# Query squares with their bias columns in two loads, and ctx of pair 1 loaded ahead of transposed ctx of pair 2

## The reference

```python
# x (8, 64, 256), ctx (8, 1601, 256)
q, k, v = ln(x) @ Wq + bq, ctx @ Wk + bk, ctx @ Wv + bv
x = x + softmax(q @ k.T / 16) @ v @ Wo + bo
Q, K, V = ln(x) @ Wq2.T + bq2, ln(x) @ Wk2.T + bk2, ln(x) @ Wv2.T + bv2
x = x + softmax(causal(Q @ K.T / 16)) @ V
h = ln(x)                                   # 512 tokens in all
raw = h @ centroids.T                       # 8 scores a token
top = the 2 experts with the largest sigmoid(raw + routing_bias)
w = softmax(sigmoid(raw)[top])
out = x + h + shared(h) + sum(w_e * expert_e(h) for e in top)
```

## Time and profile before

| | us |
|---|---|
| median of 3 runs | 250.69 |
| lowest and highest run | 250.62, 250.86 |
| span of the profiled execution | 249.0 |
| PE busy in it | 242.5 |
| DVE, ACT, POOL busy | 154.1, 138.0, 53.0 |

### The profile page before, as it was taken

The page is one execution under the profiler, slowest core; times in us unless marked ns, Lnnn a source line. Parts: engine busy times, 40 slices in busy tenths (PEclk is TensorE's granted clock), DMA queues, the critical chain, the costliest instruction groups (busy, mean ns, idle before and its releaser), DMA issues.

```text
span 249.0 us, 5101 instructions
## 1 busy us (share of the span) xinstructions
PE 242.5 (97%) x1892; PEld 209.2 (84%) x1892; DVE 154.1 (62%) x369; ACT 138.0 (55%) x274; POOL 53.0 (21%) x82
## 2 busy tenths in 40 slices
PE   8999999989999999999998999999999999999994
PEld 8757366456367599999998999999999999999994
DVE  1752363534645887789759247766676776667683
ACT  3435132052152788796776266666666666666641
POOL 3400000000100210320676002112222222136700
PEclk9999999999999999999999999999999999999999
DMA  7999999999999999940127558999998999920232
GB/s 250 417 437 416 420 396 417 398 408 420 375 388 374 320 346 437 428 184 0 68 85 240 227 195 278 357 365 352 375 371 341 371 357 348 361 90 21 53 139 84
DMA packets 14014, 74.12 MB, mean 298 GB/s; under 512 B 1540, under 2 KB 8588, under 8 KB 9644
## 3 DMA queue, kind: packets, MB, share of 16 engines
q1 hardware_dynamic: 12700, 70.59, 74.6%
q0 software_dynamic: 1008, 2.76, 3.0%
q10 hardware_dynamic: 288, 0.52, 0.6%
HBM read 67.56 MB, written 6.32 MB: 297 GB/s over the span
## 4 chain that ended last, share of the span: by engine, by line
PE 81%; DMA 12%; DVE 3%; ACT 1%; issue 1%; SPq 0%; POOL 0%; DVEq 0%; ACTq 0%
PE psum L519 68%; DMA ctx<-ctx_dram 12%; PE psum L779 7%; DVE dlo L1362 2%; PE psum L797 1%; PE psum L617 1%; PE psum L543 1%; PE psum L840 1%; PE psum L708 1%; PE psum L550 0%; ACT dhi L1006 0%; PE psum L666 0%; DVE hlo L1247 0%; SPq L341 0%; PE psum L699 0%
## 5 line engine op out<-in xcount | busy, mean ns | idle before, releaser
L519 PE MATMUL psum<-xrowT,ring 128*128 128x128 f32 x480 | 58.3, 275 | 0.0
L519 PEld LDWEIGHTS psum<-xrowT,ring 128*128 128x128 f32 x480 | 56.2, 192 | 0.0
L1362 DVE TENSOR_TENSOR dlo<-ring,dhi 128x1024 fp32r<-128x1024 f32 x30 | 38.3, 1280 | 3.8 <-ACT dhi L1006 3.8
L1381 DVE TENSOR_TENSOR slot_hlo<-slot_h,slot_hhi 128x512 fp32r<-128x512 f32 x30 | 20.8, 692 | 29.9 <-ACT slot_hhi L1034 29.9
L1032 ACT ACTIVATE slot_h<-psum 128x512 f32<-128x512 f32 x30 | 17.9, 598 | 35.1 <-PE psum L519 35.1
L519 PE MATMUL psum<-dhi,slot_hhi 128*128 128x256 f32 x120 | 36.3, 302 | 0.1
L519 PE MATMUL psum<-dhi,slot_hlo 128*128 128x256 f32 x120 | 33.8, 282 | 0.0
L519 PE MATMUL psum<-dlo,slot_hhi 128*128 128x256 f32 x120 | 33.8, 282 | 0.0
L511 POOL DMA_INDIRECT results_dram<-y_rows,result_row x13 | 17.1, 1319 | 70.5 <-DMA results_dram<-y_rows,result_row 54.0
L1006 ACT ACTIVATE dhi<-ring 128x1024 fp32r<-128x1024 f32 x30 | 31.1, 1042 | 0.0
L519 PE MATMUL psum<-xh,parted 128*128 128x256 f32 x128 | 26.9, 288 | 0.0
(11 more groups left out here) (204 smaller groups left out, 394.0 us busy)
## 6 DMA issues: line engine op xcount, KB each, us to landing
ring<-experts_dram SPq DMA_DIRECT2D x15, 2048.0 KB, 8.0
ctx<-ctx_dram SPq DMA_DIRECT2D x4, 3072.0 KB, 28.3
ctxT_start<-ctxT_start_dram SPq DMA_DIRECT2D x4, 2048.0 KB, 20.1
ctxT_rest<-ctxT_rest_dram SPq DMA_DIRECT2D x4, 1154.0 KB, 22.4
raw<-experts_dram SPq DMA_DIRECT2D x2, 2048.0 KB, 15.9
slot_x_dram<-empty_row SPq DMA_DIRECT2D x1, 1935.0 KB, 16.3
xrow<-slot_x_dram SPq DMA_DIRECT2D x15, 129.0 KB, 7.3
squares<-squares_dram SPq DMA_DIRECT2D x1, 1285.0 KB, 14.1
```

The lines of the kernel that those rows point to most:

```text
L519: return pe.matmul(out, lhsT, rhs, start=first, stop=last)
L1362: dve.tensor_tensor(dlo[b % 2][:, steps, :], ring[b][:, steps, C * P:STEP_W], dhi[b % 2][:, steps, :].bitcast(F32), ALU.subtract).then_inc ...
L1381: dve.tensor_tensor(slot_hlo[:, half, :], slot_h[:, half, :], slot_hhi[:, half, :].bitcast(F32), ALU.subtract).then_inc(slot_hlo_ready, 1)
```

## The change

Three things are done.

1. The 13 bias and centroid columns and the two query squares become one array (`queries_dram`) and one tile (`query_start`, 1054 columns), laid out as the columns, then half k = 0 of both squares, then half k = 1. Two loads fill it: the first brings the columns and half 0 (540 columns, 270 KB), the second half 1 (514 columns, 257 KB). The load of `cols` alone, in runs of 13 values, is gone. Each half has its own semaphore, and the fold waits for half k before it multiplies half k. ACT's `spread` waits for the first.
2. SP issues both loads of `ctx` of pair 1 right after `rows`, without a wait, and `ctxT` of pairs 2 and 3 after it. Before, it was `ctxT` 2, `ctx` 1, `ctxT` 3.
3. Two tiles (`prob`, `qT`) change place in memory, and the other five squares get a tile of their own.

```diff
-        cols = sb("cols", [P, C, NCOLS])
+        query_start = sb("query_start", [P, C * NCOLS + C * 2 * (D + 1)])
+        cols = query_start[:, 0:C * NCOLS].rearrange("p (c n) -> p c n", c=C)
+        query_squares = query_start[:, C * NCOLS:].rearrange("p (k s d) -> p s k d", k=C, s=2)
...
+        def square(n, k, start, stop):
+
+            return query_squares[:, n, k, start:stop] if n < 2 else squares[:, n - 2, k, start:stop]
+
...
-            sp.dma_start(squares[:, 0:2], squares_d[:, 0:2]).then_inc(query_squares_in, 16)
-            sp.dma_start(cols[:, :, :], cols_d.rearrange("(c p) n -> p c n", p=P)).then_inc(cols_in, 16)
+            begun = C * NCOLS + 2 * (D + 1)
+            sp.dma_start(query_start[:, 0:begun], queries_d[:, 0:begun]).then_inc(query_squares_in[0], 16)
+            sp.dma_start(query_start[:, begun:], queries_d[:, begun:]).then_inc(query_squares_in[1], 16)
...
             load_ctxT(0)
-            sp.dma_start(squares[:, 2:7], squares_d[:, 2:7]).then_inc(squares_in, 16)
+            sp.dma_start(squares[:, :, :, :], squares_d).then_inc(squares_in, 16)
             load_ctxT(1)
             load_ctx(0)
             sp.dma_start(rows[:, :], rows_d.partition_broadcast(P)).then_inc(rows_in, 16)
-            for t in range(1, T - 1):
-                load_ctxT(t + 1)
-                load_ctx(t)
-            load_ctx(T - 1)
+            load_ctx(1)
+            load_ctxT(2)
+            load_ctxT(3)
+            load_ctx(2)
+            load_ctx(3)
...
-            pe.wait_ge(query_squares_in, 16)
             for k in range(C):
+                pe.wait_ge(query_squares_in[k], 16)
                 for m in range(C):
-                    ins = pe.matmul(bank(0, m * D, D), squares[:, XWQT, k, m * P:(m + 1) * P], squares[:, XWKT, k, 0:D],
+                    ins = pe.matmul(bank(0, m * D, D), square(XWQT, k, m * P, (m + 1) * P), square(XWKT, k, 0, D),
                                     start=k == 0 and m == 0, stop=k == C - 1, skip_group_check=True)
...
-            pe.wait_ge(cols_in, 16)
...
-            act.wait_ge(cols_in, 16)
+            act.wait_ge(query_squares_in[0], 16)
```

More of the change, by code:

```diff
@@ L104, in plan, with build @@
     return order
-def build(nc, x_d, ctx_d, ctx_rest_d, ctxT_start_d, ctxT_rest_d, squares_d, cols_d, rows_d, experts_d, out_d, slot_x_d, results_d):
+def build(nc, x_d, ctx_d, ctx_rest_d, ctxT_start_d, ctxT_rest_d, queries_d, squares_d, rows_d, experts_d, out_d, slot_x_d, results_d):
     with ExitStack() as whole:
@@ L190, in build @@
                            sb(f"ctxT{i}_rest", [P, 2, C, KV - 2 * BANK], F32, phase1))
-            squares = sb("squares", [P, 7, C, D + 1], F32, phase1)
+            prob = sb("prob", [P, KV], F32, phase1)
+            qT = sb("qT", [P, C, N], F32, phase1)
+            squares = sb("squares", [P, 5, C, D + 1], F32, phase1)
             aq = sb("aq", [P, C, D], F32, phase1)
@@ L198, in build @@
             product = sb("product", [P, D], F32, phase1)
-            qT = sb("qT", [P, C, N], F32, phase1)
-            prob = sb("prob", [P, KV], F32, phase1)
             probT = sb("probT", [P, KT, P], F32, phase1)
@@ L260, in build @@
         LATE_BANKS = (PO, 3, CHAIN, PT + 1)
-        x_start_in, x_rest_in, squares_in, cols_in, rows_in = (
-            sem("x_start_in"), sem("x_rest_in"), sem("squares_in"), sem("cols_in"), sem("rows_in"))
-        query_squares_in = sem("query_squares_in")
+        x_start_in, x_rest_in, squares_in, rows_in = (
+            sem("x_start_in"), sem("x_rest_in"), sem("squares_in"), sem("rows_in"))
+        query_squares_in = [sem("query_start_in"), sem("query_rest_in")]
         aq_hi, aq_lo, x1_hi, x1_lo = sem("aq_hi"), sem("aq_lo"), sem("x1_hi"), sem("x1_lo")
@@ L524, in fold_vec @@
                     for k in range(C):
-                        ins = mm(bank(b, at + m, 1), squares[:, left, k, m * P:(m + 1) * P],
+                        ins = mm(bank(b, at + m, 1), square(left, k, m * P, (m + 1) * P),
                                  cols[:, k, col:col + 1], k == 0, k == C - 1)
@@ L531, in fold_row @@
                 for k in range(C):
-                    ins = mm(bank(b, 0, D + 1), bcast[:, spread, k, :], squares[:, right, k, :], k == 0, k == C - 1)
+                    ins = mm(bank(b, 0, D + 1), bcast[:, spread, k, :], square(right, k, 0, D + 1), k == 0, k == C - 1)
                 return ins
@@ L690, in chain_v @@
                 for c in range(C):
-                    ins = mm(bank(V_BANKS[t], 0, D), xn2T[:, c, :], squares[:, AWVT, c, 0:D], c == 0, c == C - 1)
+                    ins = mm(bank(V_BANKS[t], 0, D), xn2T[:, c, :], square(AWVT, c, 0, D), c == 0, c == C - 1)
                 ins.then_inc(v_ps, 1)
@@ L720, in _ @@
                 for k in range(C):
-                    ins = mm(bank(PT, m * D, D), squares[:, XWVT, k, m * P:(m + 1) * P],
-                             squares[:, XWO, k, 0:D], k == 0, k == C - 1)
+                    ins = mm(bank(PT, m * D, D), square(XWVT, k, m * P, (m + 1) * P),
+                             square(XWO, k, 0, D), k == 0, k == C - 1)
             ins.then_inc(fold_ps, 1)
@@ L725, in _ @@
                 for k in range(C):
-                    ins = mm(bank(PT + 1, m * D, D), squares[:, AWQ, k, m * P:(m + 1) * P],
-                             squares[:, AWK, k, 0:D], k == 0, k == C - 1)
+                    ins = mm(bank(PT + 1, m * D, D), square(AWQ, k, m * P, (m + 1) * P),
+                             square(AWK, k, 0, D), k == 0, k == C - 1)
             ins.then_inc(fold_ps, 1)
@@ L730, in _ @@
             for k in range(C):
-                ins = mm(bank(PO, 0, D), bcast[:, 1, k, :], squares[:, XWO, k, 0:D], k == 0, k == C - 1)
+                ins = mm(bank(PO, 0, D), bcast[:, 1, k, :], square(XWO, k, 0, D), k == 0, k == C - 1)
             ins.then_inc(fold_ps, 1)
@@ L1457 @@
                        a["L0_attn_bq"], a["L0_attn_bk"], a["L0_attn_bv"]])
-    squares = np.concatenate([squares, beside[:, :, None]], axis=2)
+    squares = np.concatenate([squares, beside[:, :, None]], axis=2).reshape(7, C, P, D + 1)
+    cols = np.concatenate([np.stack([a["L0_xattn_bq"], a["L0_xattn_bk"], a["L0_xattn_bv"],
+                                     a["L0_attn_bq"], a["L0_attn_bk"]]), a["L0_ffn_centroids"]]).T
     ctx = a["ctx_1024"].reshape(T, 2, KV, D)
@@ L1467 @@
         "ctxT_rest_dram": ctxT[..., 2 * BANK:],
-        "squares_dram": squares.reshape(7, C, P, D + 1).transpose(2, 0, 1, 3),
-        "cols_dram": np.concatenate([np.stack([a["L0_xattn_bq"], a["L0_xattn_bk"], a["L0_xattn_bv"],
-                                               a["L0_attn_bq"], a["L0_attn_bk"]]),
-                                     a["L0_ffn_centroids"]]).T,
+        "queries_dram": np.concatenate([cols.reshape(C, P, NCOLS).transpose(1, 0, 2).reshape(P, -1),
+                                        squares[0:2].transpose(2, 1, 0, 3).reshape(P, -1)], axis=1),
+        "squares_dram": squares[2:].transpose(2, 0, 1, 3),
         "rows_dram": np.concatenate([a["L0_xattn_bo"], a["L0_attn_bv"], a["L0_ffn_routing_bias"]]),
```

## The result

| | before | changed |
|---|---|---|
| median, us (6 runs each, same chips) | 251.05 | 257.57 |
| lowest to highest | 250.62 to 251.65 | 257.07 to 258.90 |
| ratio, 95% interval | | 1.0277 (1.0257 to 1.0297) |
| span of the profiled execution, us | 249.0 | 255.6 |
| PE busy in it, us | 242.5 | 243.7 |

The account below looks back on a forecast made before the run. PE was taken as the bound, busy 242.5 of 249.0 us. Span 249.0 + 4.3 (5.0 - 0.7) + 1.6 = 254.9, with 1.7 around it 256.6 us; range 254.0 to 258.0.

Parts of the forecast that it names:

- The place in the queue: Loads of pairs 1 and 2: they land in order of issue, each after the bytes ahead, at 411 GB/s.
- The two ways to work out the landing: ctxT_start of pair 2: 48.2 from the end of the queue, 47.8 by bytes; 48.0 taken.
- less 0.4 for the shorter start: ctxT_start of pair 2: lands at 47.6 instead of 48.0 because the columns' small runs are dropped; bounds 0 and 0.6.
- The stall: Ahead of the scores of pair 2: PE has nothing to do for 5.0 us, from 4.6 to 5.6.
- The clock: Scores of pair 2 and what follows: PE's clock falls in the wait, +1.6 us, middle of 1.0 and 2.2.
- the first rival: Scores of pair 2: PE waits but its clock does not fall; 250.7 + 4.3 = 255.0 us; chance 0.24.
- The wait that goes: Weighted sum of pair 1: its ctx load has already landed, so 0.7 us of waiting is saved.
- the queue does not run dry: Issue of ctx of pair 3: some 5 us later, still before ctx of pair 2 lands at 66.97; landing stays 75.7.
- The start: Columns with query squares in two loads: the earlier first half is hidden by PE's warm-up, 0 gained.
- PE's first 11 us are as before: Start of the kernel: a sign that the changed profile shows PE unchanged there.
- cover of 0.7 us for the second half: Fold at the start: second half of the squares lands at 5.6, needed near 6.3.
- The sign on PEld: Behind the wait at the scores of pair 2: loads of 128 columns take 0.2 us, not 0.1, for a while.

Follow-up runs that it names:

- swap alone: The kernel before with only the order of loads changed, ctx of pair 1 ahead of ctxT of pair 2, and the old start; 257.89 us, ratio 1.026.
- half the bytes: The changed kernel with ctx of pair 1 in two loads of 6 chunks, one on each side of ctxT of pair 2; 251.04 us, ratio 1.0005.
- ctx between the two loads: The changed kernel with ctx of pair 1 issued between ctxT_start and ctxT_rest of pair 2; 256.61 us, ratio 1.0228.
- the busy PE: The changed kernel with 20 multiplications of the identity on PE ahead of the scores of pair 2; 255.83 us, ratio 1.0176.
- start only: The changed kernel with the old order of loads, leaving the two-part start and the tiles that changed place; 251.16 us, ratio 1.001.
- the kernel that removed that one too: The changed kernel with old load order, ctx of pair 1 split 3 chunks first, 7 warm-up multiplications, DVE's first split behind the norms; 249.86 us, ratio 0.9955.

## Why the prediction was right and where it was wrong

*The place in the queue: right; the landing 0.4 too early.* It said that the load that PE needs first lands after the bytes put ahead of it. The swap alone, half the bytes, and ctx between the two loads each moved the wait as the bytes say. The two ways to work out the landing gave 48.2 and 47.8, and their middle, 48.0, is what came: 47.97 in the changed kernel, 47.94 in the swap alone. The step that failed is "less 0.4 for the shorter start". ctxT_start of pair 0 did land 0.3 earlier (10.65 and not 10.98), but ctxT_start of pair 2 landed no earlier with the new start than with the old one. One execution of each kernel was profiled, and with the busy PE the same order of loads landed at 48.45, so a saving of 0.3 could hide in such differences; no run shows it. The scores began at 48.09 and not 47.7: that term of the sum was mis-sized by 0.4.

*The stall: too short, by 0.75.* It was put at 5.0 from PE's time at the scores before, 42.73; it was 5.75, because in this execution PE was there at 42.34. That part costs nothing, since the landing sets the end; in the sum against the earlier trace rows it cancels.

*The clock: right that it falls, the term mis-sized by 0.5.* Predicted 1.6, the middle of 1.0 and 2.2, measured 2.1. No run shows the term, or the 1.0 and 2.2 that it lies between: they are the author's estimate, made before any run had work behind a fall. In its place the runs showed a clock of 0.50 that ran on with PE at work and cost half of that work's time. In the changed kernel this was 48.09 to 52.32, 4.23 us, and the scores took 5.73 and not 3.65. In the swap alone it was 48.07 to 52.67, 4.60 us, and the same scores took 5.91, a cost of 2.3 and so over the 2.2. With ctx between the two loads it was 50.87 to 53.77, 2.90 us, and the cost was 1.4. The busy kernel, with the clock at 1.00, took 255.83 and so 0.8 more than the 255.0 of the first rival: 0.4 lies in the median of the kernel before, the rest fits a landing that came later than the 47.6 of the sum.

*The wait that goes: right.* 0.7 predicted, 0.85 between starts, of which the bracket before showed 0.67. Nothing was earned back behind, as predicted: PE's waits from 76 us on are the same one as in the earlier trace rows. But one reason given for it failed. It said that the queue does not run dry before ctx of pair 3 is issued. That issue came at 64.85, 6.6 us later than before, when little was left to move: a DMA share of 0.19 at 50 GB/s.

```profile
64.00:66.00 2.00, 1.84 (x16) 1.17 (x13) 0.48 (x1) 0.57 (x2) 0.00 (x0) 1.00 0.19 50
```

ctx of pair 3 landed at 64.85 + 11.3 = 76.15, 0.5 later than before. It cost nothing only because its user, at 86.59, stood 10 us behind.

*The start: worth nothing, as said, though it changed more than said.* The x tile came 1.0 us earlier (DVE's first statistics at 4.24 and not 5.24), which the prediction did not see; no effect on the time followed (start only: 251.16 against 251.05). SP's first load, issued at 0.77, is about half as large now, 270 KB and not 514; whether that is the reason, no run tested. And "PE's first 11 us are as before" was wrong in the profiled execution:

```profile
1.09 3.94 PEld L527 LDWEIGHTS psum<-sm 128*128 128x128 f32 x20 [1.09 <-DVE sm L1100]
...
4.24 0.43 DVE L1084 BATCH_NORM_STATS2 stats<-xs 128x6 f32<-128x256 f32 x1 [3.21 <-DMA xs<-x_in_dram]
...
10.78 1.94 PE L527 MATMUL psum<-ctxT_start,qT 128*64 128x512 f32 x8 [0.31 <-DMA ctxT_start<-ctxT_start_dram]
```

The warm-up loads took 3.94 us and not 4.34 in this execution, and the first scores met a load that had just landed. The start-only kernel shows that no gain follows from the start by itself. The cover of 0.7 us for the second half was thin: with half of ctx ahead, where the warm-up loads took only 3.67 us, PEld waited 0.52 us for it.

*The sum.* Predicted 5.0 + 1.6 - 0.7 = 5.9 us, measured 6.6 in span and 6.5 in medians (257.57 - 251.05). Both mis-sized terms, 0.4 for the landing and 0.5 for the clock, erred to the small side, and 0.15 of the wait at the weighted sum the other way. The time forecast, 256.6, was 1.0 short of the median: 0.6 by the sum, and 0.4 because it stood on three runs of the kernel before with a median of 250.69, where all six have 251.05.

*The steps that failed* are two terms of the sum: the 0.4 taken off the landing, where the runs show nothing, and the 1.6 for the clock, where they show 2.1. The stated range, 254.0 to 258.0, holds the median, but two of the six runs, 258.70 and 258.90, lie above it, and the ratio with its interval puts the changed kernel at 257.5 to 258.5 on 251.05: the upper end was too low, since the clock cost 2.3 in the swap alone, more than the 2.2 allowed for it, and the kernel before stood 0.4 higher.

A part of the spread among the runs goes with the clock. The mean granted clock of the six is 0.984 to 0.987 in those of 257.57, 257.58, 258.70 and 258.90 us and 0.993 in those of 257.07 and 257.56. With ctx between the two loads it is 0.993 in the run of 255.62 and 0.985 in the other four, 256.59 to 257.04. As 0.984 goes with 257.58 as well as with 258.70, the clock is not all of it; the rest was not taken apart.

*The signs.* The wait of some 5 us at the scores, the early landing of ctx of pair 1 and the constant shift came as announced. The chain of waits does not name the load; it has 5.75 us of "issue" there, and only issue plus time to landing names it. The sign on PEld could not show as written: the weight loads at the clock of 0.50 have 64 columns (0.13 us each and not 0.07), and the first ones of 128 columns, at 53.75, come when it is at 1.00 again (0.10 us each).

```profile
42.34 5.75 issue
...
48.97 0.26 PEld L527 LDWEIGHTS psum<-ctxT_start,qT 128*64 128x64 f32 x2 [0.59 <-issue]
...
53.75 0.20 PEld L673 LDWEIGHTS psum<-ident,xn 128*128 128x128 f32 x2 [0.81 <-issue]
```

## What to carry to other kernels

In a queue of loads that was never empty (here a DMA share of 1.01 from 34 to 58 us in the kernel before) an earlier issue gained a load only a place, and the bytes put ahead of another load made it later: ctxT_start of pair 2 landed at 39.83 with no ctx of pair 1 ahead, at 43.42 with half of it, at 47.97 with all. So in such a queue sort the loads by when their users stand on the engine's queue, not by when their buffers are free. A wait of PE can cost more than its length: behind the stalls of 4.12, 5.25 and 5.75 us seen here its work began at a clock of 0.50, which cost 1.4 to 2.3 us more; cut the load that is ahead in two (251.04 us here and not 257.57), or give PE work (255.83). And follow a saved wait to the end of the queue: here it came back at 83 us, where the next thing was held by the same stream of loads, and only the kernel that removed that one too was faster by more than 0.2%.

## What the runs showed of the hardware that was not expected

- SP's issue of a load can take long: the 130 KB of ctx_rest took 5.66 us to issue at 9.05 and ctxT_rest 5.49 at 19.26 in the changed kernel, where in the kernel before each took under 1.1. In both issues of the changed kernel more loads had been issued ahead of them than at the same time before; whether that is the cause was not tested. SP had nothing urgent behind them here, but a load that must be issued soon would have waited.
- The time of PE's first weight loads differs between executions, though the granted clock reads 1.00 beside them in all: the 20 warm-up loads took from 3.67 to 4.34 us in the nine profiled executions with ten multiplications, 4.34 in five of them, with the old start and with the new.
- A fall of the clock from 1.00 to 0.50 was seen in stalls of 4.12, 5.25 and 5.75 us; in those of 0.86 and 1.25 us it stayed at 1.00.
